# Graph attention: the edge scaling goes from ScalarE to VectorE, and the second projection and the score rows take other places in the order

## What is computed

```python
def gat_layer(x, W, att_src, att_dst, bias, src, dst, heads, out_ch, concat):
    h = (x @ W.T).reshape(n, heads, out_ch)
    a_src = jnp.einsum('nhc,hc->nh', h, att_src)
    a_dst = jnp.einsum('nhc,hc->nh', h, att_dst)
    e = jax.nn.leaky_relu(a_src[src] + a_dst[dst], 0.2)
    m = jax.ops.segment_max(e, dst, num_segments=n)
    ex = jnp.exp(e - m[dst])
    denom = jax.ops.segment_sum(ex, dst, num_segments=n)
    alpha = ex / (denom[dst] + EPS)
    out = jax.ops.segment_sum(alpha[:, :, None] * h[src], dst, num_segments=n)
    ...
h = gat_layer(x, W1, att_src1, att_dst1, b1, src, dst, heads=8, out_ch=128, concat=True)
h = jax.nn.relu(h)
out = gat_layer(h, W2, att_src2, att_dst2, b2, src, dst, heads=1, out_ch=768, concat=True)
```

## Time and profile before

| | before |
|---|---|
| median of 3 runs | 2000.97 us (2000.8 to 2004.27) |
| the profiled execution's own time | 2000.8 us |
| its span, first to last instruction | 1998.9 us |
| busy in the span: PE, DVE, ACT, POOL | 1862.9, 1292.3, 934.8, 154.5 us |
| mean granted TensorE clock | 0.965 of full speed |

### The profile page before, as it was taken

The page is one execution under the profiler, slowest core; times in us unless marked ns, Lnnn a source line. Parts: engine busy times, 40 slices in busy tenths (PEclk is TensorE's granted clock), DMA queues, the critical chain, the costliest instruction groups (busy, mean ns, idle before and its releaser), DMA issues.

```text
span 1998.9 us, 30899 instructions
## 1 busy us (share of the span) xinstructions
PE 1862.9 (93%) x12197; PEld 1769.2 (89%) x12198; DVE 1292.3 (65%) x2466; ACT 934.8 (47%) x1543; POOL 154.5 (8%) x129
## 2 busy tenths in 40 slices
PE   5997998899999999788679999999999999999998
PEld 4885788899889999788679999999999999999998
DVE  6997766545345646888873764356565666676886
ACT  2321222324233535878543233336555666666775
POOL 0000000004000003333110000000101001001010
PEclk8997999999999989899889999999999999999999
DMA  3110002101122211110212132255656657676795
GB/s 116 48 48 1 24 25 97 38 24 49 48 72 88 72 38 46 69 38 17 95 51 87 49 103 72 71 187 194 206 202 212 216 213 239 232 259 233 286 327 195
DMA packets 36796, 234.30 MB, mean 117 GB/s; under 512 B 5916, under 2 KB 7318, under 8 KB 14632
## 3 DMA queue, kind: packets, MB, share of 16 engines
q1 hardware_dynamic: 31318, 217.41, 30.4%
q0 software_dynamic: 2656, 8.99, 2.0%
q10 hardware_dynamic: 2674, 5.87, 0.8%
HBM read 221.91 MB, written 10.35 MB: 116 GB/s over the span
## 4 chain that ended last, share of the span: by engine, by line
PE 45%; issue 6%; DVE 3%; ACT 2%; DMA 1%; POOL 0%; ACTq 0%; POOLq 0%; DVEq 0%
PE bank L2682 8%; PE bank L341 7%; PE bank L342 7%; PE bank L343 7%; PE bank L2683 3%; PE bank L2694 3%; PE bank L2698 2%; PE bank L2686 2%; PE bank L2695 2%; PE bank L2697 1%; PE bank L2685 1%; DVE weight_lo L314 1%; PE bank L2643 0%; PE bank L2032 0%; DMA weight_raw_fifth<-in_ffn_w 0%
## 5 line engine op out<-in xcount | busy, mean ns | idle before, releaser
L314 DVE TENSOR_TENSOR weight_lo<-weight_raw,weight_hi 128x2304 fp32r<-128x2304 f32 (+1 forms) x155 | 392.3, 2535 | 46.1 <-ACT weight_hi L304 45.9
L304 ACT ACTIVATE weight_hi<-weight_raw 128x2304 fp32r<-128x2304 f32 (+1 forms) x155 | 323.2, 2087 | 71.4 <-DMA weight_raw<-in_ffn_w 50.8
L341 PE MATMUL bank<-xT_hi,weight_hi 128*128 128x320 f32 (+1 forms) x576 | 182.6, 317 | 1.9 <-DVE xT_lo L362 1.8
L342 PE MATMUL bank<-xT_lo,weight_hi 128*128 128x320 f32 (+1 forms) x576 | 177.8, 309 | 0.0
L343 PE MATMUL bank<-xT_hi,weight_lo 128*128 128x320 f32 (+1 forms) x576 | 177.6, 308 | 0.0
L341 PE MATMUL bank<-weight_hi,xT_hi 128*128 128x384 f32 (+1 forms) x480 | 161.9, 337 | 7.9 <-DVE xT_lo L362 4.5
L3056 DVE TENSOR_TENSOR hidden_tmp<-hidden_tmp,bank 128x160 f32<-128x160 f32 (+5 forms) x192 | 65.7, 342 | 159.1 <-ACT hidden_tmp L2842 159.1
L342 PE MATMUL bank<-weight_lo,xT_hi 128*128 128x384 f32 (+1 forms) x480 | 157.5, 328 | 0.0
L343 PE MATMUL bank<-weight_hi,xT_lo 128*128 128x384 f32 (+1 forms) x480 | 157.3, 328 | 0.0
L665 PE MATMUL bank<-one_hot_dst,one_hot_src 125*128 125x313 f16 x800 | 122.9, 305 | 15.2 <-ACT packed_counts L679 7.9
L2842 ACT ACTIVATE hidden_tmp<-bank,ffn_b_by_load 128x160 f32<-128x160 f32 (+5 forms) x192 | 73.6, 404 | 121.0 <-PE bank L2686 118.8
(11 more groups left out here) (499 smaller groups left out, 5078.9 us busy)
## 6 DMA issues: line engine op xcount, KB each, us to landing
weight_raw<-in_ffn_w SPq DMA_DIRECT2D x111, 1152.0 KB, 5.2
weight_raw_fifth<-in_ffn_w SPq DMA_DIRECT2D x25, 1152.0 KB, 5.3
weight_raw<-in_shared_w SPq DMA_DIRECT2D x16, 1152.0 KB, 5.1
weight_raw<-in_mix_kv SPq DMA_DIRECT2D x8, 1152.0 KB, 5.2
weight_raw<-in_gat_w SPq DMA_DIRECT2D x8, 768.0 KB, 4.2
weight_raw<-in_mix_q SPq DMA_DIRECT2D x4, 1152.0 KB, 5.0
weight_raw<-in_mix_out SPq DMA_DIRECT2D x4, 1152.0 KB
weight_raw<-in_gnn_w SPq DMA_DIRECT2D x4, 1152.0 KB, 5.1
```

The lines of the kernel that those rows point to most:

```text
L304: act.activation(upper_, whole_, ACT.Copy).then_inc(*w_hi.one())
L314: dve.tensor_tensor(lower_, whole_, upper_.bitcast(F32), ALU.subtract).then_inc(*w_lo.one())
L341: pe.matmul(dst, a[0], b[0], start=first, stop=False)
L342: pe.matmul(dst, a[0], b[1], start=False, stop=False)
```

## The change

Three things change, all in `graph_attention`:

1. The scaling by the factor. ScalarE's activation L2211 goes; VectorE's last small step L2364 (factor times `has_edge`) becomes a tensor_scalar over the unit's 128x640 edges with the factor and `has_edge` as two per-row scalars. The edges are thus scaled at lag 3 instead of lag 4; TensorE turns the unit at lag 5 as before.
2. The second projection y leaves its table. It is made where the second head of a pair of tiles has reached lag 9, for all tiles of the pair at once: tiles 0 and 1 in tick 12, 2 and 3 in tick 16, 4 in tick 18 after the group's first, for every group. The copies and dot products of the last group's h2 follow at lags 9 and 10.
3. "turned" and "spread" join `PREPARE`: at the end of ticks 8 and 9 of each ten instead of within ticks 9 and 10.

```diff
-        PREPARE = {6: (0, 1), 7: (2, 3), 8: (4,)}
-        Y_AT = {10 * grp + tick: (grp, t) for grp in range(4) for t, tick in enumerate((12, 13, 18, 19, 21) if grp < 3 else (12, 13, 16, 17, 18))}
-        TURNED = {grp * 10 - 1: grp for grp in range(1, 4)}
-        SPREAD = {grp * 10: grp for grp in range(1, 4)}
+        PREPARE = {6: (0, 1), 7: (2, 3), 8: (4, "turned"), 9: ("spread",)}
...
@@ tensor @@
-                if i in Y_AT:
-                    grp, t = Y_AT[i]
-                    q = 6 * grp + 2 * (t // 2) + 1
+                q = pair_closing(i, 9)
+                if q is not None and pairs_of[q][1] == 1:
+                    grp, _, t0, n = pairs_of[q]
                     w = weight("gat_w2", grp)
                     pe.wait_ge(*z_lo.at(q + 1))
-                    a0 = (t % 2) * P
-                    for c in range(2):
-                        bank = ring.next(y_added.at(len(y_banks) + 1))
...
+                    for a in range(n):
+                        for c in range(2):
+                            bank = ring.next(y_added.at(len(y_banks) + 1))
...
-                if i in TURNED:
-                    source_rows_turned(TURNED[i])
-                if i in SPREAD:
-                    source_rows_spread(SPREAD[i])
@@ scalar @@
-                u = unit(i, 4)
-                if u is not None:
-                    grp, h, t = units[u][0:3]
-                    e = edge_w[:, u % ZS, :]
-                    act.wait_ge(*e_summed.at(u + 1))
-                    act.activation(e, e, ACT.Copy, scale=total[:, grp % 2, h, t:t + 1]).then_inc(*e_scaled.one())
...
-                if i in TURNED:
-                    rows_turned(TURNED[i])
-                if i in SPREAD:
-                    rows_spread(SPREAD[i])
...
-                if i - 1 in Y_AT and Y_AT[i - 1][0] == 3:
-                    t = Y_AT[i - 1][1]
+                q = pair_closing(i, 10)
+                if q is not None and pairs_of[q][0:2] == (3, 1):
+                    _, _, t0, n = pairs_of[q]
+                    for t in range(t0, t0 + n):
...
@@ vector @@
+                    e = edge_w[:, u % ZS, :]
                     tot = total[:, grp % 2, h, t:t + 1]
                     dve.wait_ge(*e_exp.at(u + 1))
                     own_step(dve.tensor_scalar(tot, tot, 1e-16, None, ALU.add))
                     own_step(dve.reciprocal(tot, tot))
-                    dve.tensor_tensor(tot, tot, has_edge[:, t:t + 1], ALU.mult).then_inc(*e_summed.one())
+                    dve.tensor_scalar(e, e, tot, has_edge[:, t:t + 1], ALU.mult, ALU.mult).then_inc(*e_scaled.one())
...
+                q = pair_closing(i, 10)
+                if q is not None and pairs_of[q][0:2] == (3, 1):
+                    _, _, t0, n = pairs_of[q]
+                    for t in range(t0 + 1, t0 + n):
+                        second_scores(t)
+                q = pair_closing(i, 9)
+                if q is not None and pairs_of[q][1] == 1:
+                    grp, _, t0, n = pairs_of[q]
+                    for t in range(t0, t0 + n):
...
                     if grp == 3:
-                        second_scores(t)
+                        second_scores(t0)
                 for grp, step in preparations(i):
                     prepare(grp, step)
-                if i in TURNED:
-                    rows_turned(TURNED[i])
```

More of the change, by code:

```diff
@@ L1845, in graph_attention @@
          att_in, h_full, h_hi, h_lo, scored, score_turned, score_hi, score_lo, rows_full, rows_kept,
-         e_acted, e_made, e_exp, e_summed, e_scaled, ex_turned, ex_hi, ex_lo, z_full, z_relu, z_hi, z_lo,
+         e_acted, e_made, e_exp, e_scaled, ex_turned, ex_hi, ex_lo, z_full, z_relu, z_hi, z_lo,
          y_full, y_added, scored2, h2_hi, h2_lo, o_full, o_added) = sigs(*names)
@@ L2058, in tensor @@
             for i in range(N1 + LAST_LAG):
-                if i in Y_AT:
-                    grp, t = Y_AT[i]
-                    q = 6 * grp + 2 * (t // 2) + 1
+                q = pair_closing(i, 9)
+                if q is not None and pairs_of[q][1] == 1:
+                    grp, _, t0, n = pairs_of[q]
                     w = weight("gat_w2", grp)
                     pe.wait_ge(*z_lo.at(q + 1))
-                    a0 = (t % 2) * P
-                    for c in range(2):
-                        bank = ring.next(y_added.at(len(y_banks) + 1))
-                        y_banks.append(bank)
-                        product(bank[:, 0:HALF], [(at(zT, ALL, z_slot(q), k, slice(a0, a0 + P)), at(w, ALL, k, slice(c * HALF, (c + 1) * HALF)))
-                                                  for k in range(2)]).then_inc(*y_full.one())
+                    for a in range(n):
+                        for c in range(2):
+                            bank = ring.next(y_added.at(len(y_banks) + 1))
+                            y_banks.append(bank)
+                            product(bank[:, 0:HALF], [(at(zT, ALL, z_slot(q), k, slice(a * P, (a + 1) * P)), at(w, ALL, k, slice(c * HALF, (c + 1) * HALF)))
+                                                      for k in range(2)]).then_inc(*y_full.one())
                 q = pair_closing(i, 7)
@@ L2197, in scalar @@
                     upper(at(zT, ALL, z_slot(q), h, slice(0, n * P)), zt[:, q % 2, 0:n * P]).then_inc(*z_hi.one())
-                if i in Y_AT and Y_AT[i][1] == TT - 1:
-                    grp = Y_AT[i][0]
+                q = pair_closing(i, 9)
+                if q is not None and pairs_of[q][1:3] == (1, TT - 1):
+                    grp = pairs_of[q][0]
                     weight_read[w2_chunk(grp)] = y_full.at(10 * (grp + 1))
@@ L2225, in scalar @@
                     weight_hi(SPLIT[i])
-                if i - 1 in Y_AT and Y_AT[i - 1][0] == 3:
-                    t = Y_AT[i - 1][1]
[L2228 to L2231, removed]
+                q = pair_closing(i, 10)
+                if q is not None and pairs_of[q][0:2] == (3, 1):
+                    _, _, t0, n = pairs_of[q]
+                    for t in range(t0, t0 + n):
+                        act.wait_ge(*y_added.at(2 * (3 * TT + t) + 2))
+                        if t == 0:
+                            act.wait_ge(*h_full.at(4 * TT))
+                        upper(at(hp, ALL, t, ALL), h2[:, t, :]).then_inc(*h2_hi.one())
             rows_turned(4)
@@ L2367, in vector @@
                     peak(u, *units[u][0:3])
[L2368 to L2379, removed]
+                q = pair_closing(i, 10)
[3 more added lines that the diff above has]
+                        second_scores(t)
+                q = pair_closing(i, 9)
+                if q is not None and pairs_of[q][1] == 1:
+                    grp, _, t0, n = pairs_of[q]
+                    for t in range(t0, t0 + n):
+                        for c in range(2):
+                            i_y = 2 * (grp * TT + t) + c
+                            o = h2[:, t, c * HALF:(c + 1) * HALF]
+                            dve.wait_ge(*y_full.at(i_y + 1))
+                            if grp == 0:
+                                dve.wait_ge(*x_kept.at(16))
+                                dve.tensor_copy(o, y_banks[i_y][:, 0:HALF]).then_inc(*y_added.one())
+                            else:
+                                dve.wait_ge(*y_added.at(i_y - 2 * TT + 1))
+                                dve.tensor_tensor(o, o, y_banks[i_y][:, 0:HALF], ALU.add).then_inc(*y_added.one())
                     if grp == 3:
-                        second_scores(t)
+                        second_scores(t0)
                 for grp, step in preparations(i):
                     prepare(grp, step)
-                if i in TURNED:
-                    rows_turned(TURNED[i])
                 if i in SPLIT:
```

2 lines of the change are left out of this document (1 added, 1 removed).

## The result

The changed kernel took 2013.35 us (median of 5 runs, 2012.36 to 2015.86), the kernel before 2003.87 us in the runs beside it (5 runs, 2000.8 to 2006.62). The ratio is 1.0054, 95% interval [1.004, 1.0067]: 0.54% of 2003.87, or about 10.8 us slower (the two medians differ by 9.5 us). Forecast was slower by 6.5 us. The profiled execution after took 2008.69 us with a span of 2006.8 us, 7.9 us more than before; it is the second fastest of 14 executions of the changed kernel, which lie between 2007.78 and 2016.9 us.

What follows compares the result with a forecast made beforehand. It saw no single bound: ScalarE paced most windows, but VectorE's queue mostly ended TensorE's waits. Terms -1.0 + 1.5 + 1.8 + 1.0 + 2.2 + 1.0 + 0 = +6.5 us on 2000.8 gave 2007.3 us, range 1998.5 to 2014.5.

Steps and rivals of the forecast that it cites:

- stretch 3: Loop turns (ticks) 16 to 20: +1.8 us, from TensorE's queue with more y products and the early "turned".
- tail: After tick 39 to the stage's end: 0 us, bounds -3 and +3.
- The scale's price: VectorE's new 128x640 tensor_scalar: 0.61 us long, step 0.52 us, so +0.40 us per tick.
- Cheap and dear scale: Rivals on VectorE's added step: 0.40 gives 2003.2 us (chance 0.26 with free schedule); 0.75 gives 2015 (0.15 with stalling bursts).
- ScalarE's relief: ScalarE loses 40 activations with a step of about 0.72 us, some 29 us.
- Relief decides: Rival: ScalarE's lost work sets the time if GpSimd's holds miss VectorE; 1994 to 1997 us, chance 0.14.
- The hold-up by GpSimd: GpSimd's edge terms delay VectorE's scale right after the peak by 0.5 us; some 5 us of the sum.
- Stretch 1: Up to tick 10: -1.0 us, as most of TensorE's 2.5 us wait for scaled edges goes.
- stretch 6: Ticks 31 to 39: +1.0 us, in VectorE's queue with and without holds by GpSimd.
- Stretch 2, 4 and 6: Ticks 11 to 15, 21 to 25 and 31 to 39: +1.5, +1.0 and +1.0 us, summed as VectorE's queue.
- Stretches 3 and 5: Ticks 16 to 20 and 26 to 30: +1.8 and +2.2 us, from y and "turned" in TensorE's queue.
- The sign at L362: TensorE's waits for the lower halves made by VectorE, 13.4 us before, would rise by several us.

Runs made afterwards that it cites:

- e8: Kernel before with the 128x640 scaling left out altogether: stage 3.7 us shorter; total 3616.01 us, ratio 1.8061, says nothing of the edit.
- e1: Kernel before with only the scaling moved to VectorE: 2007.22 us, ratio 1.0024, stage +4.2 us.
- e7: Changed kernel with GpSimd's edge terms cut to 16 of 640 columns after unit 2: 1999.03 us, ratio 0.9987 to the kernel before.
- e9: Kernel before with the edge terms cut to 16 of 640 columns after unit 2, as a control: 1999.7 us, ratio 0.9987.
- e10: Changed kernel with the 128x1 product separate again and the scale also summing its row, unread: 2021.47 us, ratio 1.0094 to the kernel before.
- e3: Kernel before with only "turned" and "spread" moved to the ends of ticks 8 and 9: 2012.66 us, ratio 1.0047.
- e4: Kernel before with the scaling on VectorE and y in its new places, score rows as before: 2014.5 us, ratio 1.0061.
- e11: Kernel before with y and the score rows in their new places, scaling still on ScalarE: 2013.55 us, ratio 1.0057.
- e5: Changed kernel with 16 unread filler matmuls ahead of the early score rows: 2015.15 us, ratio 1.0065 to the kernel before.
- e6: Kernel before with unread filler matmuls in TensorE's longest pauses, in the loop and ahead of the second layer: 1999.94 us, ratio 0.9988.
- e12: Kernel before with unread filler matmuls only late, from tick 38 and ahead of the second layer: 2000.7 us, ratio 0.999.

## Why the prediction was right or wrong

The direction and the engine were right, the size was not: +6.5 forecast, +9.4 in the stage and about +10.8 timed.

- **TensorE's clock** is the step that failed. The sum took it as it was: stretch 3 is worked out "at the clock it had", and only the tail has bounds for it, around a term of 0. From tick 1 to 45, TensorE was busy at the lower level for 39.2 us before and 48.0 after. By the rate above, these 8.8 us are 3.4 to 4.4 of the stage's 9.4, more than the 2.9 by which the forecast missed it. The times say the same. The two executions of the changed kernel at 0.963 took 2007.78 and 2008.69 us, the twelve at 0.958 to 0.960 2012.36 to 2016.9. At the clock of before the change would cost 4 to 6.5 us, an estimate with the two slopes above. So the forecast is about right for a clock that stays, and the clock did not stay. This is an argument from sums: no run holds the clock, and why it fell more often isn't shown.
- **The scale's price** was right: 0.614 us for 0.61, step 0.53 (881.30 to 881.83) for 0.52. Cheap and dear scale are both refuted as such.
- **ScalarE's relief**: e8 bounds it at 3.7 us. "Relief decides" put the total 4 to 7 us below before; leaving the scaling out altogether gives 3.7. That it fell is shown, and so is why: VectorE's ends, more than ScalarE's, released TensorE. From e8 to e1 VectorE's share of the scaling alone costs 3.7 + 4.2 = 7.9 us.
- **The hold-up by GpSimd** was seen rightly: without it the loss is gone (e7). Its size, "some 5 us" of the sum, looks too small beside the 9.5 us that e7's stage is shorter. But 1.8 of these lie in the second layer, behind the last term of the sum. Up to the peak of tick 41 e7 is 7.7 us shorter, with 35.2 us at the lower level for after's 41.5. By the rate above that is 2.5 to 3.2, and 4.5 to 5.2 are left for the holds, by estimate what was forecast. That VectorE, busy 22.32 of 24 us, has lost the slack that covered the old holds would also explain why e9 gave 1.5 us and e7 9.5, but the unlike clocks explain most of that difference too, so this is not shown. The rule of the Trainium skill that I weighed (SBUF — State Buffer, Who interferes with whom) holds here, with 611 ns free and up to 1773 held; the same section excepts the form that writes its accumulator, and e10 agrees.
- **Stretch 1** had the wrong sign, +1.4 for -1.0. I had costed the early rows for the later groups only. Those made in tick 8 put the peaks of ticks 9 and 10 2.7 and 3.2 us late (2.5 and 3.7 in e3, 0.1 and 0.5 in e1), and TensorE was busy at the lower level for 10.3 us here, 3.9 before. The longer wait in tick 8, 4.2 us for 2.8, is the scaling's: it stands in e1 and not in e3. Nor did "most of the 2.5 us" of the earlier trace rows lie here: one of the two waits, 1.0 us, is at 942.67 us, in stretch 6.
- **Stretch 2, 4 and 6**: +1.6, +1.4, +1.2 for +1.5, +1.0, +1.0. Without the holds (e7) 6 comes to -0.1, and but for 0.7 us in after no kernel of the three was at the lower level there, so it is the holds. Stretch 2 comes to -0.4, but there e7 had no low clock at all, for 5.8 us before and 6.5 after, so holds and clock are not separated. In 4 e7 had 5.5 us of it for 2.8, which can hide what the holds gave back.
- **Stretches 3 and 5**: +2.9 and +3.6 for +1.8 and +2.2. The three waits at L1995 of 2 us or more came as forecast, two of them of 2.14 for 2.2. Stretch 3 falls to +0.6 in e7, although e7 has the same low-clock spell behind its wait (spread 2.97, z 3.42 us); so there the clock is not the cause of the excess and the holds are. Stretch 5 stays at +3.6 in e7: here the holds are not the cause. It had 7.4 us at the lower level for 5.2 before, by the rate above some 1 of the 1.4 us beyond the forecast.
- **Tail**: -2.6 for 0, inside its bounds of 3. Before had z and y at the lower clock here (3.12 and 4.15 us at 971 to 978 us); after had a z at 964.6 to 968.1 us and the end of its last y, from 992.1 us, there. At the lower level the tail had 17.9 us before and 14.4 after.
- **The sign at L362** came in another form: TensorE's waits for it fell from 13.4 to 8.5 us, while those put down to the weight split L314, ahead of it in the same queue, rose from 2.7 to 11.1.
- **What adds to what** was not asked in the prediction: it summed parts, and e1 to e4 and e11 show that the three parts don't sum.

Open: what makes TensorE's clock fall in one pause and not in the other (e5 against e6 and e12), and how much of the loss is left when it doesn't. The timed loss (10.8) is larger than the stage's (9.4) at least in part because the profiled execution ran at 0.963 and most of the timed ones at 0.960 or less.

## What to carry to other kernels

Before the gains of one edit in two kernels are compared, compare the granted clocks of their runs. Here 1.5 us and 9.5 us looked like holds that cost nothing in one kernel and everything in the other; brought to a like clock they are, by estimate, 5.5 to 6.6 and 6.3 to 8.6. A forecast for a kernel that TensorE bounds needs a term for its clock, with bounds, wherever the change opens or moves a pause. Work moved to VectorE where GpSimd runs is to be costed with its holds, though how much of them shows in the time depends on what waits for VectorE. Whether an engine that is busy 94% of the time is the bound is told by what ends the waits, and most cheaply by leaving its work out (here 29 us of work were worth 3.7). And parts of a schedule that uncover the same wait are not to be summed.

## What the runs showed of the hardware

- A VectorE instruction was held only if it started while GpSimd's 128x640 add ran, and if both inputs lay in SBUF (L314, L2299, gat_zT_lo, the 128x1 product L2364) or it was the plain 128x640 tensor_scalar. Those that read a PSUM bank (L2255 at 0.42 us, 6 times under GpSimd's op in after) and the scale with a sum (0.88) kept their time.
- It goes both ways: a weight split begun first kept GpSimd's add at 3.11 us instead of 1.56. So freeing one instruction can move the hold to a worse place (e10).
- Filler matmuls before the second layer kept TensorE at the upper clock (first product 5.56 us in e12, 8.19 before); 16 of them in a 2-us pause of the loop did not (e5).
- At the lower clock z took 3.33 us for 2.04, the spread 2.98 for 1.40. Executions of one kernel differ in it: the changed kernel's mean granted clock lay between 0.958 and 0.963, and its time between 2016.9 and 2007.78 us.
